# Layer 0's 64 slots written out on four engines, layer 1's left in its loop

## The chip, the core and the metric

The kernel runs on one core of a Trainium2 chip. The metric is the device time of one execution in microseconds (us). Five engines work side by side, each on its own list of instructions: TensorE (PE in the rows; PEld is its weight load), VectorE (DVE), ScalarE (ACT), GpSimd (POOL) and SyncE (SP), which issues most of the transfers. They meet only through semaphores.

## The reference, cut to what matters

Two transformer layers work on 1,024 tokens of width 256 (4 sequences of 256), all in fp32. Layer 0 is attention with 16 query heads and 8 key/value heads, an RMS norm and a rotation of queries and keys and a window of 128, and then a feed-forward part that keeps 2 of every 4 hidden values. Layer 1 is causal attention with 16 heads, and then a feed-forward part with a Walsh-Hadamard transform.

```python
x = x + _L0_attn_ref(_layernorm(x), ...)   # 16 heads in 8 pairs, 4 sequences
x = x + _L0_ffn_ref(_layernorm(x), ...)
x = x + _L1_attn_ref(_layernorm(x), ...)   # 16 heads in 8 pairs, 4 sequences
x = x + _L1_ffn_ref(_layernorm(x), ...)
```

## The kernel before

The attention of a layer is cut into 64 units: 8 pairs of heads, and in each pair 8 units (4 sequences times 2 heads). A **slot** c is one step of a software pipeline: in it every engine works on several units at once. In slot c TensorE makes the scores of unit c, projects tile c+5 of the weights (six matmuls with 512 columns, L535 in layer 0, L543 in layer 1), multiplies the probabilities of an earlier unit with the values (L465, L470, L472) and makes the output product of unit c-6 (L427). VectorE adds outputs to `x` (L734 or L743), takes the maxima of the scores (L798), splits results into a high and a low fp32r part (L754, L762, L810, L812, L859) and turns the probabilities in blocks of 32 (L774). ScalarE takes the exponentials (L713), copies results out of PSUM (L621, L635 to L639, L664, L675 to L699), and in layer 1 makes the high part of the turned probabilities (L591) and issues the transfer of the blocks (L603). GpSimd splits weights (L888, L890) and in layer 0 does a part of the rotation (L901 to L910).

Nobody schedules this at run time: each engine's list is written in the order of its slot function (`pe_slot`, `act_slot`, `dve_slot`, `pool_slot`), and waits on semaphores tie the lists together. The function `slots` (L949) writes the slots of a layer: slots -5 to 8 one after the other, then a hardware loop (`eng.Fori`, L954) with a body of 16 slots that runs 3 times (slots 9 to 56), then the rest. So each of the four engines has a loop for layer 0 and one for layer 1, with two jumps back each. In a loop the number that a wait compares with depends on the pass, so that `need` (L70 to 76) and `need_pairs` (L79 to 84) make a register operation ahead of such a wait; outside a loop it is a constant. SyncE's list has no loop in either layer.

`Fori` itself leaves rows at L954: a register set ahead of the loop (MOVE), the loop's first instruction (FUSED_REGOPS), and at its end an addition (ALU_OP) and the jump (COMPARE_BRANCH).

The sizes of the loops, counted in the built program with waits and register operations (the accumulator reads that the trace shows on ScalarE and the weight loads of TensorE included), and the place of their first and last instruction in the engine's list, counted from 0:

| engine | whole list | layer 0's loop | layer 1's loop |
|---|---|---|---|
| PE | 4,993 | 444 to 1232 (789) | 2776 to 3748 (973) |
| DVE | 1,365 | 190 to 481 (292) | 875 to 1144 (270) |
| ACT | 1,333 | 203 to 566 (364) | 871 to 1163 (293) |
| POOL | 464 | 96 to 271 (176) | 373 to 425 (53) |
| SP | 730 | none | none |

Of the kernel before, what the change touches and what calls it, by code (L numbers as in the profile page):

```python
# [36 lines left out]
UNITS = 8 * PAIRS  # L37
# [11 lines left out]
FIRST_SLOT, LOOP_FROM, LOOP_STEP, LOOPS, LAST_SLOT = -5, (9, 9), 16, 3, 70  # L49
FIRST_TAIL = UNITS - 8 + 7  # L50
# [56 lines left out]
def build(nc, x_in, wa, wax, wb, wdown0, w2t, consts, scales, shuffle, out):  # L107
    with ExitStack() as ctx:
# [839 lines left out]

        def slots(eng, L, body, head, tail):  # L949

            for c in range(FIRST_SLOT, LOOP_FROM[L]):
                body(eng, L, None, c)
                head(c)
            with eng.Fori(0, LOOPS) as it:  # L954
                for j in range(LOOP_STEP):
                    body(eng, L, it, LOOP_FROM[L] + j)
            for c in range(LOOP_FROM[L] + LOOP_STEP * LOOPS, (LAST_SLOT if L else UNITS - 1) + 1):
                body(eng, L, None, c)
                tail(c - FIRST_TAIL)

# [729 lines left out]
        @block.gpsimd  # L1690
        def _(pool):
            nc.gpsimd.memset(zero[:, :], 0.0).then_inc(s_zero, 1)
            nc.gpsimd.memset(neg_half[:, :], -0.5).then_inc(s_half, 1)
            nc.gpsimd.memset(rms_eps[:, :], RMS_EPS).then_inc(s_half, 1)
            pool.wait_ge(s_zero, 1)
            pool.wait_ge(s_half, 2)
            for t in range(2):
                ln_pool(pool, 0, t)
            pool.wait_ge(s_rope, 16)
            pool.wait_ge(s_scl, 16)  # L1700
            for a in (2, 0):
                if a == 0:
                    pool.wait_ge(s_scq, 1)
                nc.gpsimd.tensor_tensor(cos_t[:, :, a, :], cos_c, scl[:, a // 2, :].unsqueeze(1).broadcast_to([P, 2, DH]),
                                        ALU.mult).then_inc(s_cos, 1)
            ln_pool_two(pool, 0, 2)
            pool_b(pool, 0, None, 0, 0)
            slots(pool, 0, pool_slot, pool_head0, pool_tail(pool, 0))
            pool_drain0(pool)
            for t in range(4):  # L1710
                ln_pool(pool, 2, t)
            slots(pool, 1, pool_slot, pool_head, pool_tail(pool, 1))
            for n in range(2, 5):
                pool_piece_lo(pool, 1, n)
            for n in range(5, len(pieces[1])):
                if pieces[1][n][0] == "b1" and pieces[1][n - 1][0] == "b0":
                    pool.wait_ge(ff[1]["lo"], 4)
                pool_piece(pool, 1, n)
# [4 lines left out]
        def _(act):  # L1723
# [8 lines left out]
            for L in range(2):  # L1732
# [20 lines left out]
                def tail(t):  # L1753
# [10 lines left out]
                    if L == 1 and t == 7:  # L1764
                        act_function_ahead(act, ACT.Silu)

                slots(act, L, act_slot, head, tail)
                if L == 0:
                    act_drain0(act)
# [219 lines left out]
```

## Time and profile before

| what | value |
|---|---|
| time, median of 3 runs | 686.02 us (684.66 to 689.99) |
| the profiled execution | 690.5 us, its span 688.7 us |
| busy: PE, DVE, ACT, POOL | 664.8, 559.8, 445.0, 361.8 us |
| mean granted TensorE clock | 0.988 of full speed |

The profile shows one execution. A span runs from the first to the last instruction of the program. Layer 0's attention lies at about 21 to 262 us, layer 1's at about 357 to 605 us; the feed-forward parts stand behind each.

### The profile page before, as it was taken

The page shows a single profiled execution, that of the slowest core. Times are in us where ns is not written, and L with a number is a line of the kernel's source. Part 1 is how long each engine was busy: PE and PEld are TensorE (multiplying, and loading weights), DVE is VectorE, ACT ScalarE, POOL GpSimd, SP SyncE. Part 2 cuts the span into 40 slices and gives each one's busy share as a digit, 9 for nine tenths or more (in the row PEclk, how much of TensorE's full clock was granted, in tenths as well). Part 3 has the DMA queues.
Part 4 walks back from the last instruction along what each step waited for, and adds up shares of the span by engine and source line. Part 5 has one row for each costly group of instructions (what it writes and reads, how often), then busy time and mean ns, then how long its engine had stood idle before and what let it go on. Part 6 is the DMA issues. An engine that isn't in the chain of part 4 may idle for free.

```text
span 688.7 us, 16131 instructions
## 1 busy us (share of the span) xinstructions
PE 664.8 (97%) x4153; PEld 591.8 (86%) x4153; DVE 559.8 (81%) x1706; ACT 445.0 (65%) x1721; POOL 361.8 (53%) x557
## 2 busy tenths in 40 slices
PE   7999997999799998999998999999999999999998
PEld 4689996899699997888887999999999999978887
DVE  6988996899689978878866999889899988796433
ACT  4899996899689976431435676666666666764222
POOL 5999997899789973201148943425152324027000
PEclk9999999899899999999999999999999999999999
DMA  7156574666456551100024667565656655100000
GB/s 244 48 116 147 135 159 103 140 146 128 101 122 144 124 168 49 48 0 1 16 91 86 134 134 160 110 152 111 155 117 140 135 122 130 40 1 1 1 31 31
DMA packets 242574, 69.27 MB, mean 101 GB/s; under 512 B 184400, under 2 KB 238544, under 8 KB 242384
## 3 DMA queue, kind: packets, MB, share of 16 engines
q1 hardware_dynamic: 219280, 56.53, 37.2%
q10 hardware_dynamic: 23232, 12.06, 5.9%
q8 instruction: 21, 0.34, 0.2%
q14 instruction: 41, 0.34, 0.2%
HBM read 45.29 MB, written 23.27 MB: 100 GB/s over the span
## 4 chain that ended last, share of the span: by engine, by line
PE 83%; DVE 7%; issue 4%; ACT 2%; POOL 1%; DMA 1%; SPq 0%; DVEq 0%; ACTq 0%; POOLq 0%
PE bank L543 12%; PE bank L1003 12%; PE bank L427 11%; PE bank L535 11%; PE bank L564 6%; PE bank L395 5%; PE bank L470 4%; PE bank L388 4%; PE bank L472 4%; PE bank L1077 3%; PE bank L465 3%; PE bank L487 3%; PE bank L1081 3%; DVE x L743 1%; PE bank L1097 1%
## 5 line engine op out<-in xcount | busy, mean ns | idle before, releaser
L713 ACT ACTIVATE probs<-scores,negmax 128x128 f32<-128x128 f32 (+1 forms) x256 | 117.4, 473 | 16.0 <-DVE negmax L798 15.6
L621 ACT CAST enc_hi<-bank 128x256 fp32r<-128x256 f32 x128 | 48.7, 380 | 78.4 <-PE bank L472 74.7
L888 POOL TENSOR_TENSOR a_hi<-raw_a,zero 128x384 fp32r<-128x384 f32 (+1 forms) x60 | 44.9, 749 | 73.0 <-PE bank L564 73.0
L325 POOL TENSOR_TENSOR ln_r<-ln_ve,neg_half 128x1 f32<-128x1 f32 x26 | 17.0, 655 | 118.4 <-DVE ln_ve L299 118.4
L427 PE MATMUL bank<-b_hi,enc_hi 128*128 128x256 f32 x256 | 77.9, 304 | 0.5 <-DVE x L743 0.5
L774 DVE STREAM_TRANSPOSE blocks<-probs 128x384 f32<-128x384 f32 x113 | 64.8, 573 | 12.2 <-ACT probs L713 9.4
L427 PE MATMUL bank<-b_hi,enc_lo 128*128 128x256 f32 x256 | 72.1, 282 | 0.0
L427 PE MATMUL bank<-b_lo,enc_hi 128*128 128x256 f32 x256 | 71.8, 281 | 0.0
L906 POOL TENSOR_TENSOR rot_a<-rot_a,rot_b 128x384 f32<-128x384 f32 x64 | 65.2, 1019 | 8.7 <-DVE rot_b L875 8.5
L743 DVE SCALAR_TENSOR_TENSOR x<-bank,rinv,x 128x256 f32<-128x256 f32 x144 | 67.4, 468 | 2.3 <-PE bank L427 1.0
L754 DVE TENSOR_TENSOR enc_lo<-bank,enc_hi 128x256 fp32r<-128x256 f32 x128 | 53.3, 416 | 18.7 <-PE bank L395 10.1
L904 POOL TENSOR_TENSOR rms_r<-meansq,neg_half 128x3 f32<-128x3 f32 x64 | 54.8, 856 | 7.6 <-POOL meansq L901 3.8
L1160 ACT ACTIVATE gate<-bank 128x512 f32<-128x512 f32 x32 | 19.1, 598 | 58.7 <-PE bank L1003 57.9
L890 POOL TENSOR_TENSOR a_lo<-raw_a,a_hi 128x384 fp32r<-128x384 f32 (+1 forms) x60 | 53.7, 896 | 4.7
L535 PE MATMUL bank<-a_hi,xT_hi 128*128 128x512 f32 x128 | 52.3, 411 | 2.6 <-DVE rot_b L875 1.3
L713 ACT ACTIVATION_READ_ACCUMULATOR probs<-scores,negmax 128x1 f32 x256 | 54.1, 211 | 0.0
L543 PE MATMUL bank<-xT_hi,a_hi 128*128 128x512 f32 x128 | 52.3, 409 | 0.3 <-DVE xT_lo L352 0.3
L661 ACT ACTIVATE gate<-bank 128x128 f32<-128x128 f32 x192 | 50.7, 282 | 1.7 <-PE bank L535 1.7
L427 PEld LDWEIGHTS bank<-b_hi,enc_hi 128*128 128x128 f32 x256 | 48.5, 189 | 3.4 <-issue 0.9
L535 PE MATMUL bank<-a_hi,xT_lo 128*128 128x512 f32 x128 | 50.8, 399 | 0.0
L543 PE MATMUL bank<-xT_lo,a_hi 128*128 128x512 f32 x128 | 50.7, 396 | 0.0
L535 PE MATMUL bank<-a_lo,xT_hi 128*128 128x512 f32 x128 | 50.7, 399 | 0.0
(186 smaller groups left out, 2339.7 us busy)
## 6 DMA issues: line engine op xcount, KB each, us to landing
arrived<-shuffle SPq DMA_DIRECT2D x452, 48.0 KB, 2.2
shuffle<-blocks ACTq DMA_DIRECT2D x57, 192.0 KB, 2.5
shuffle<-blocks SPq DMA_DIRECT2D x56, 192.0 KB, 2.1
raw_a<-in_wa SPq DMA_DIRECT2D x40, 192.0 KB, 3.2
raw_b<-in_wb SPq DMA_DIRECT2D x16, 256.0 KB, 2.9
raw_a<-in_wa SPq DMA_DIRECT2D x32, 128.0 KB, 2.8
hid_last<-in_wax SPq DMA_DIRECT2D x2, 512.0 KB, 3.8
w_a<-in_w2t SPq DMA_DIRECT2D x1, 1024.0 KB, 4.9
```

Source lines behind the costliest of these rows:

```text
L427: mm = pe.matmul(output_bank(L, m)[:, cols], enc[l][:, h, t * P:(t + 1) * P], b_w[slot][r][:, h * D:(h + 1) * D], start=i == 0 and not (on ...
L535: mm = pe.matmul(ps[:, :], xT[l][:, g, t * P:(t + 1) * P], a_w[slot][r][:, g * 512:(g + 1) * 512], start=i == 0, stop=i == 5)
L543: mm = pe.matmul(ps[:, :], a_w[slot][l][:, g * 768 + w * P:g * 768 + (w + 1) * P], xT[r][:, g, half * 512:(half + 1) * 512], start=i == 0, ...
L661: nc.scalar.activation(gate[:, m % 2, a * DH:(a + 1) * DH], bank[PJ_BANK + m % 2][:, a * DH:(a + 1) * DH], ACT.Square, scale=float(DH) ** ...
L713: nc.scalar.activation(probs[:, c % 4, c0:c1], scores[:, c % 2, c0:c1], ACT.Exp, bias=negmax[:, c % 2, r:r + 1], scale=-1.0, accum_out=row ...
L743: nc.vector.scalar_tensor_tensor(out=x[:, m % 8, :], in0=output_bank(L, m)[:, hh * D:(hh + 1) * D], scalar=rinv[:, u, r:r + 1], in1=x[:, m ...
L754: nc.vector.tensor_tensor(enc[1][:, w % 2, dst], bank[O_BANK][:, 0:D], enc[0][:, w % 2, dst].bitcast(F32), ALU.subtract).then_inc(s["elo"], 1)
L774: nc.vector.transpose(blocks[:, c % 2, :], probs[:, c % 4, :]).then_inc(s_blocks[L], 1)
L890: nc.gpsimd.tensor_tensor(lo, src, hi.bitcast(F32), ALU.subtract).then_inc(s_lo, 1)
L904: nc.gpsimd.tensor_tensor(rms_r[:, t, :], meansq[:, m % 2, :], neg_half[:, 0:3], ALU.pow).then_inc(s["rp"], 1)
L906: nc.gpsimd.tensor_tensor(rot_a[:, m % 2, :], rot_a[:, m % 2, :], rot_b[:, m % 2, :], ALU.add).then_inc(s["radd"], 1)
L1003: mm = pe.matmul(ps[:, :], a_w[t][l][:, c0:c0 + P], xT[rr][:, g, th * 512:(th + 1) * 512], start=q == 0, stop=q == 5)
```

## The change

In layer 0, `slots` writes out slots -5 to 63 one after the other, with the same slot functions and the same head and tail functions around them; there is no loop, and each wait compares with a constant. Layer 1 goes through the code of before. The change touches the lists of TensorE, VectorE, ScalarE and GpSimd.

```diff
         def slots(eng, L, body, head, tail):
 
+            if L == 0:
+                for c in range(FIRST_SLOT, UNITS):
+                    body(eng, 0, None, c)
+                    if c < LOOP_FROM[0]:
+                        head(c)
+                    else:
+                        tail(c - FIRST_TAIL)
+                return
             for c in range(FIRST_SLOT, LOOP_FROM[L]):
                 body(eng, L, None, c)
                 head(c)
             with eng.Fori(0, LOOPS) as it:
                 for j in range(LOOP_STEP):
                     body(eng, L, it, LOOP_FROM[L] + j)
-            for c in range(LOOP_FROM[L] + LOOP_STEP * LOOPS, (LAST_SLOT if L else UNITS - 1) + 1):
+            for c in range(LOOP_FROM[L] + LOOP_STEP * LOOPS, LAST_SLOT + 1):
                 body(eng, L, None, c)
                 tail(c - FIRST_TAIL)
```

The tail functions do nothing before slot 63 but for GpSimd's, which works at slot 62 as before. The lists of the changed kernel, counted in the same way:

| engine | whole list | layer 0's loop | layer 1's loop |
|---|---|---|---|
| PE | 6,417 | none | 4200 to 5172 (973) |
| DVE | 1,815 | none | 1325 to 1594 (270) |
| ACT | 1,925 | none | 1463 to 1755 (293) |
| POOL | 683 | none | 592 to 644 (53) |
| SP | 730 | none | none |

VectorE's list where layer 0's loop begins (slot 9), before. ISA at L954 is the loop's first instruction; ISA and REGISTER_ALU at L74 are register operations of waits; waits alone are not listed.

```order
L954 UNCONDITIONAL_BRANCH
L954 ISA
L74 ISA
L74 REGISTER_ALU
L734 TENSOR_TENSOR x<-bank,x 128x256
L798 ISA scores,negmax<-bank,cst,rms_r 128x128
L798 ISA negmax 128x1
L798 ISA scores,negmax<-bank,cst,rms_r 128x256
L798 ISA negmax 128x1
```

The same list where one slot of layer 0 follows another, now.

```order
L780 RECIPROCAL rinv<-rowsum 128x2
L754 TENSOR_TENSOR enc_lo<-bank,enc_hi 128x256
L734 TENSOR_TENSOR x<-bank,x 128x256
L798 ISA scores,negmax<-bank,cst,rms_r 128x128
L798 ISA negmax 128x1
L798 ISA scores,negmax<-bank,cst,rms_r 128x256
L798 ISA negmax 128x1
```

The loop's instruction, its jump and the register operations are gone, and the operations stand in the order of before.

VectorE's list at the end of layer 0's loop, before:

```order
L774 STREAM_TRANSPOSE blocks<-probs 128x384
L74 REGISTER_ALU
L869 TENSOR_TENSOR rot_a<-bank,cos_t 128x384
L875 TENSOR_TENSOR rot_b<-bank,sin_t 128x384
L74 REGISTER_ALU
L780 RECIPROCAL rinv<-rowsum 128x2
L754 TENSOR_TENSOR enc_lo<-bank,enc_hi 128x256
L954 REGISTER_ALU
L954 COMPARE_AND_BRANCH
```

Now these operations stand as in the fence above it, with the next slot's behind them. In layer 1 nothing changes but the loop's place in the list and its line (L962 in the changed file).

## Rows read from the trace of the kernel before

**Rows 1.** The page: busy time by engine, granted clock in 40 slices, instruction queues.
```profile
PE 664.8 (97%) x4153; PEld 591.8 (86%) x4153; DVE 559.8 (81%) x1706; ACT 445.0 (65%) x1721; POOL 361.8 (53%) x557
...
PEclk9999999899899999999999999999999999999999
...
q14 instruction: 41, 0.34, 0.2%
```
**Rows 2.** Windows of time: length, busy us (instructions) by engine, clock, DMA share, GB/s.
```profile
52.20:107.20 55.00, 55.00 (x362) 50.23 (x362) 49.46 (x172) 50.42 (x240) 51.02 (x88) 1.00 0.66 145
107.20:125.30 18.10, 13.96 (x74) 12.06 (x73) 10.34 (x37) 10.38 (x48) 13.34 (x24) 0.81 0.47 103
176.40:190.30 13.90, 9.95 (x51) 8.71 (x50) 7.00 (x24) 6.96 (x32) 9.41 (x17) 0.75 0.41 90
390.30:584.90 194.60, 194.60 (x1375) 181.69 (x1374) 176.47 (x544) 128.11 (x455) 75.87 (x108) 1.00 0.60 133
```
**Rows 3.** Timeline, TensorE in layer 0: start us, us, line, operation, [idle before <- releaser].
```profile
107.14 0.39 PE L388 MATMUL bank<-qk 128*128 128x128 f32 x2
118.81 0.87 PE L487 MATMUL bank<-cst,rot_a 128*128 128x128 f32 x3 [3.99 <-DVE k_parts L812]
125.30 0.39 PE L388 MATMUL bank<-qk 128*128 128x128 f32 x2
176.38 0.44 PE L388 MATMUL bank<-qk 128*128 128x128 f32 x2
190.27 0.39 PE L388 MATMUL bank<-qk 128*128 128x128 f32 x2
```
**Rows 4.** The chain that ended last, at layer 0's first jump: start us, us, what.
```profile
110.88 0.06 DVEq L954
110.94 3.25 issue
114.19 0.06 DVEq L954
114.25 2.50 issue
```
**Rows 5.** The same chain at layer 0's second jump.
```profile
176.54 2.85 issue
179.45 2.40 issue
```
**Rows 6.** Line L954 in layer 1, 455 to 458 us: count, durations, first start.
```profile
L954 ACTq COMPARE_BRANCH  x1: 50/50/50, 455.7 to 455.7; - x1
L954 ACTq FUSED_REGOPS  x1: 50/50/50, 455.9 to 455.9; - x1
L954 DVEq COMPARE_BRANCH  x1: 63/63/63, 456.6 to 456.6; - x1
L954 DVEq FUSED_REGOPS  x1: 63/63/63, 456.9 to 456.9; - x1
```
**Rows 7.** Line L954 in layer 0, 110 to 118 us, ScalarE.
```profile
L954 ACTq COMPARE_BRANCH  x1: 54/54/54, 110.0 to 110.0; - x1
L954 ACTq FUSED_REGOPS  x1: 50/50/50, 110.3 to 110.3; - x1
```
**Rows 8.** Instruction packets (number, MB, share), 110 to 118.5 us.
```profile
q14 instruction: 3, 0.02, 1.1%
```
**Rows 9.** The same, 458 to 584 us.
```profile
q14 instruction: 1, 0.01, 0.0%
```
**Rows 10.** Timeline of a slot in layer 1 behind its first jump.
```profile
458.32 0.38 ACT L675 COPY qk<-bank 128x256 f32<-128x256 f32 x1
458.59 0.60 ACT L680 CAST k_gate<-bank 128x512 fp32r<-128x512 f32 x1
459.64 0.69 DVE L859 TENSOR_TENSOR k_last<-bank,k_gate 128x512 fp32r<-128x512 f32 x1
462.34 0.40 PE L543 MATMUL bank<-xT_hi,a_hi 128*128 128x512 f32 x1
```

## The prediction
> **What bounds the kernel now.** I read the page first. TensorE is busy 97% of the span and VectorE 81% [rows 1], so a gain has to come out of TensorE's idle time or its clock. The strip of the granted clock dips in a few slices only, two of them in layer 0's attention. Windows of time show why these two matter [rows 2]. From 52.2 to 107.2 us TensorE is busy 55.00 of 55.00 us at full clock. From 107.2 to 125.3 us it is busy 13.96 of 18.10 at a mean clock of 0.81, and from 176.4 to 190.3 us 9.95 of 13.90 at 0.75. In layer 1's slots, 390.3 to 584.9 us, it is busy all the time at full clock. So layer 0 has two holes and layer 1 has none.
>
> The timeline sizes the holes [rows 3]. A slot begins with the matmul at L388. From 125.30 to 176.38 us there are 14 slots, 3.65 us each. From 107.14 to 125.30 there are three in 18.16 us, which is 7.2 us more than 10.95. From 176.38 to 190.27 there are two in 13.89 us, 6.6 more than 7.30. In the first hole TensorE sat idle for 3.99 us waiting for VectorE (L812); what is left of the 7.2 is mostly its lower clock after that wait, the 1.2 GHz level for a part of the window.
>
> The chain of waits names the cause [rows 4, 5]. At 110.88 us stands VectorE's jump back (L954), then 3.25 us in which it waited for nothing that the profile shows, then the loop's first instruction, then 2.50 us more of the same, and only then its second. At the second jump the two gaps are 2.85 and 2.40 us. At these moments instruction packets arrive: three between 110 and 118.5 us [rows 8]. So VectorE waits for its own code.
>
> **Why there and not elsewhere.** Length alone does not decide. ScalarE's loop in layer 0 has 364 instructions and takes 0.3 us from jump to first instruction [rows 7]; VectorE's has 292 and pays 5.9. In layer 1 VectorE (270) and ScalarE (293) take 0.2 to 0.3 us [rows 6], and over the next two passes one packet arrives [rows 9]. Place does decide, by this working. The 41 packets of queue 14 have 8 KB each [rows 1]. The four lists other than TensorE's hold 3,892 instructions (the table of lists), and some are fetched again in the loop, about ten packets; 3,892 by 31 is 126, so I take 128 to a packet, an estimate. VectorE's first instruction after the jump (190) ran alone and the second waited for another packet, so a block edge lies between 190 and 191, and then at every 128th: 319, 447, 575 and so on. Layer 0's loop (190 to 481) touches four blocks, with 1, 128, 128 and 35 instructions; layer 1's (875 to 1144) three. With the same edges ScalarE's loops (203 to 566, 871 to 1163) touch three each. The one with four stalls, and those with three don't: as if four blocks stay, one of them the block ahead.
>
> **The change part by part.**
>
> 1. Layer 0's jumps go, on all four engines. Worth 7.2 + 6.6 = **13.8 us**, idle time and clock together. The slot pace of 3.65 us stays: TensorE is busy throughout [rows 2] and its matmuls don't change. The register operations of the waits go too; I cost them at nothing, since TensorE's work hides them.
>
> 2. Code that is written out has to be fetched as well. VectorE's 48 slots become about 740 instructions, six blocks in 175 us. Before, between 52.2 and 107.2 us, the lists also crossed block edges with TensorE busy throughout [rows 2]; a block is asked for while the one before it runs. I take 0; the bound above is the second gap of a jump, 2.50 us at each edge [rows 4].
>
> 3. Layer 1's loops keep their length and move in their lists, which the diff does not show. VectorE's goes to 1325 to 1594; the edges are 1343, 1471 and 1599, so three blocks, with 4 instructions to spare. I take 0. ScalarE's goes to 1463 to 1755; the edges are 1471, 1599 and 1727, so **four blocks**, with 8, 128, 128 and 29 instructions. That is the shape that stalls. So ScalarE should now stall at layer 1's two jumps.
>
> What does that cost? It resumes 3.31 us after the jump and reaches its ninth instruction 2.57 later (the gaps of [rows 4] with the instructions between). The jump is at 455.7 [rows 6], so that is 461.5 instead of about 458.3. The copies that free the projection's bank, L675 and L680, come 3.2 us late, ending at 462.4. VectorE's L859 (0.69) behind them ends at 463.1 instead of 460.3, and the next projection on TensorE, due at 462.34 [rows 10], waits 0.8. With the shorter gaps of [rows 5] it is 0.3. If ScalarE's edge lies an instruction earlier, its copy at L621 is late too and each grows by about 0.8. What is late next is the sent blocks, by about 3 us with three slots of 4 us to go. I take **1 us a jump, 2 in all**. The bounds: 0, since nothing in layer 1 is removed that could give a gain, and 6.9 a jump, which is what a stall with no slack cost in layer 0.
>
> Sum against the profiled execution: 690.5 - 13.8 + 2 = 678.7 us. That execution lies 4.5 us above the median of the runs, 686.02, so the forecast for the median is 686.0 - 11.8 = **674.2 us**.
>
> **Rivals.**
>
> A. Layer 1 stays free, because ScalarE's edges lie elsewhere: 686.0 - 13.8 = 672.2 us. Against it: ScalarE's 364 instructions fit three blocks only if an edge lies at most 20 before instruction 203, and from nearly all such places layer 1's loop now touches four. The Trainium skill speaks for this rival ("Runtime: NRT & Kernel Launch", section "Instruction fetch mechanics"): code is fetched straight ahead, mostly hidden, and only a taken branch to a place no longer held stalls, so writing loops out is preferred. By it alone the sum ends at 672.2. It counts blocks of 256 instructions, of which two are held; by that VectorE's 270 of layer 1 could not stay, but they take 0.3 us here [rows 6], so its sizes don't fit this trace. Chance 15%.
>
> B. ScalarE's stall falls on TensorE with a larger part, up to 6.9 a jump: 674 to 686, with 680 as its middle. For it: in the first hole a wait of 3.99 us brought the lower clock with it. Against: between L859's end and L543 there are 2.0 us of slack [rows 10], and in layer 1 ScalarE is busy only 128 of 195 us [rows 2]. Chance 12%.
>
> C. Slower than before: VectorE's loop of layer 1 touches a fourth block too. Four instructions to spare decide it: if the engine reads five ahead at the jump, the block behind is asked for and the first is lost. Then both engines fetch twice at each jump, on one queue; one behind the other that is up to 11 us, less 2.0 of slack, plus the 2.9 (6.9 less 4.0) that the clock and the restart took in layer 0, so 12 a jump: 686.0 - 13.8 + 24 = 696 us. Side by side it is 6.9 a jump and 686. Against: the gap behind layer 0's jump shows an instruction at a block's end running before the next block is there [rows 4]. Chance 7%, half on each side.
>
> D. The written-out code waits at its block edges: six on VectorE at 2.5 us is 15, so 686.0 - 13.8 + 2 + 15 = 689 us. Against: the crossings of before show nothing [rows 2]. Chance 4%.
>
> The forecast keeps 62%.
>
> **How the numbers follow.** The predicted time is the forecast's, 674.2. The forecast's own range is 671 to 678: ScalarE's price from 0.3 to about 3 a jump, and the spread of the runs. Rival A lies within it; B reaches to 686. A range of 670 to 681 holds the forecast, A, and the lower half of B, some 80% once the misses at its ends are taken off. 1% is 6.9 us, about what a measurement here can tell from no change: faster means below 679.2, slower above 692.9. The forecast, A and half of B, less a little for what I have not seen, give 0.80 faster; the rest of B, half of C and D give 0.15 within 1%; the rest of C and the unseen give 0.05 slower.
>
> **What would show it.** Step 1: between layer 0's head and its last slots, TensorE is busy throughout at full clock, slots stand 3.65 us apart, and the chain has no gap at a jump. Step 2: no idle time of VectorE or ScalarE that nothing explains, though packets arrive all along. Step 3: at layer 1's jumps ScalarE's first instruction comes about 3 us after its jump, with another gap within the next ten instructions; VectorE's comes within 0.3 us; TensorE loses about a microsecond in the slot after. ScalarE free at layer 1's jumps proves my edges wrong (A); gaps on VectorE there mean C; TensorE's clock falling there means B. The prediction as a whole is wrong if layer 0's pace gets longer than 3.65 us without the loop, which no row here leads me to expect.

## The result, and the profile after

The changed kernel takes 677.1 us (median of 4 runs, 676.3 to 679.2) where the kernel before, run beside it, takes 686.6 (684.7 to 690.0): a ratio of 0.986 with a 95% interval of 0.982 to 0.991. A later set of six runs gave 0.986 [0.983, 0.989], 676.5 against 686.2 us. The forecast was 674.2 with a range of 670 to 681. The profiled execution of the changed kernel took 676.3 us.

The page of the changed kernel, against [rows 1]: busy time by engine, granted clock in 40 slices, instruction queues.

```profile
span 674.5 us, 15574 instructions
...
PE 659.0 (98%) x4153; PEld 586.6 (87%) x4153; DVE 554.6 (82%) x1705; ACT 446.2 (66%) x1721; POOL 360.0 (53%) x557
...
PEclk9999999999999999999999999999999999999999
...
q14 instruction: 50, 0.41, 0.2%
```

No slice dips any more. Queue 14 brought 50 packets where it brought 41. The four lists other than TensorE's are 1,261 instructions longer, about ten packets of code; the ten or so that were fetched again in layer 0 are gone, and about as many are fetched again in layer 1 (experiments 1 and 2 show both).

Windows of time, as in [rows 2]: layer 0's slots first, then layer 1's.

```profile
52.20:228.00 175.80, 175.80 (x1153) 160.63 (x1151) 159.59 (x551) 161.35 (x769) 164.59 (x287) 1.00 0.65 142
376.00:566.00 190.00, 188.04 (x1323) 174.68 (x1322) 168.55 (x521) 124.86 (x439) 76.64 (x109) 1.00 0.60 132
```

Layer 0's two holes are gone: TensorE is busy 175.80 of 175.80 us at full clock. Its pace is not quite the 3.65 us of before, though: from about 136 us on, every second slot takes some 3.71, 0.9 us in all. There GpSimd waits for nothing, and its operations of two slots take 7.36 us, where two of TensorE's slots at 3.65 take 7.30:

```profile
194.62 0.39 PE L388 MATMUL bank<-qk 128*128 128x128 f32 x2
...
198.33 0.39 PE L388 MATMUL bank<-qk 128*128 128x128 f32 x2
...
193.93 0.61 POOL L888 TENSOR_TENSOR a_hi<-raw_a,zero 128x256 fp32r<-128x256 f32 x1
...
201.29 0.62 POOL L888 TENSOR_TENSOR a_hi<-raw_a,zero 128x256 fp32r<-128x256 f32 x1
```

In the slot between the two matmuls GpSimd's L910 ends at 197.89 us, and the weight load of L487, which reads its result, starts at 197.94. Layer 1, which had none in [rows 2], now leaves TensorE idle for 1.96 us. Where that lies, the records of the loop's own line around layer 1's first jump tell (count, durations in ns, first and last start in us; [rows 6] has the same of before):

```profile
L962 ACTq COMPARE_BRANCH  x1: 54/54/54, 438.9 to 438.9; - x1
...
L962 DVEq COMPARE_BRANCH  x1: 68/68/68, 439.8 to 439.8; - x1
...
L962 DVEq FUSED_REGOPS  x1: 63/63/63, 440.2 to 440.2; - x1
L962 ACTq FUSED_REGOPS  x1: 56/56/56, 441.9 to 441.9; - x1
```

VectorE resumes 0.35 us behind its jump as before, ScalarE 2.96 us behind its own, where it took 0.2. The chain of waits (start us, us, what) shows ScalarE there:

```profile
439.61 2.27 issue
441.88 0.06 ACTq L962
...
442.71 0.37 ACT enc_hi L621
443.08 1.72 issue
...
444.94 0.07 ACT qk L675
...
445.23 0.11 ACT k_gate L680
...
446.08 0.89 ACT probs L713 x4
...
447.20 0.07 DVE blocks L774
...
447.70 0.44 DVE x L743
...
448.81 0.95 PE bank L427 x6
```

Two gaps, as the forecast had them: one before the loop's first instruction and 1.72 us after its eighth. What follows is a longer train than the forecast followed: the exponentials (L713) are late, behind them VectorE's turn of the probabilities (L774), behind that the output added to `x` (L743), and TensorE's L427 needs the bank that L743 frees. TensorE's timeline has both waits (columns as in [rows 3]):

```profile
441.04 0.39 PE L388 MATMUL bank<-qk 128*128 128x128 f32 x2
...
445.02 0.39 PE L388 MATMUL bank<-qk 128*128 128x128 f32 x2
...
446.68 0.47 PE L543 MATMUL bank<-xT_hi,a_hi 128*128 128x512 f32 x1 [0.92 <-DVE k_last L859]
...
448.81 0.36 PE L427 MATMUL bank<-b_hi,enc_hi 128*128 128x256 f32 x1 [0.53 <-DVE x L743]
...
450.88 0.39 PE L388 MATMUL bank<-qk 128*128 128x128 f32 x2
...
510.42 0.39 PE L388 MATMUL bank<-qk 128*128 128x128 f32 x2
...
513.30 0.36 PE L427 MATMUL bank<-b_hi,enc_hi 128*128 128x256 f32 x1 [0.49 <-DVE x L743]
515.38 0.39 PE L388 MATMUL bank<-qk 128*128 128x128 f32 x2
```

A slot of 3.98 us becomes one of 5.86 (445.02 to 450.88): 1.9 us lost. At the second jump ScalarE's gaps are shorter, 2.51 and 1.28 us, the wait for L859 is gone and only that at L427 is left; the slot takes 4.96, 1.0 us lost.

**Where the time came from.** I measure a layer from its first to its last score matmul (L388) in the timelines. The profile of before that stands ahead of the prediction has 239.4 us in layer 0 and 245.6 in layer 1. A second profile of before, taken for this comparison (685.3 us, near the median), has 237.4 and 242.0. The changed kernel has 226.1 and 244.9. Against the second profile that is 11.3 us less in layer 0 and 2.9 more in layer 1, together 8.4; the spans differ by 9.0, and 0.6 lies elsewhere.

### The profile page after: what moved, and what is told of

Read it like the earlier page. It is cut to its first block, busy times and chain, and to the rows that moved or that the text cites. A ratio compares the mean times of both kernels' runs of the same rounds, so it can differ in the third digit from the quotient of the medians.

```text
span 674.5 us, 15574 instructions
## 1 busy us (share of the span) xinstructions
PE 659.0 (98%) x4153; PEld 586.6 (87%) x4153; DVE 554.6 (82%) x1705; ACT 446.2 (66%) x1721; POOL 360.0 (53%) x557
## 4 chain that ended last, share of the span: by engine, by line
PE 85%; DVE 6%; issue 4%; ACT 3%; POOL 1%; ACTq 0%; DVEq 0%; POOLq 0%
PE bank L543 12%; PE bank L1011 12%; PE bank L427 12%; PE bank L535 11%; PE bank L564 6%; PE bank L395 5%; PE bank L470 4%; PE bank L472 4%; PE bank L388 4%; PE bank L1085 3%; PE bank L487 3%; PE bank L465 3%; PE bank L1089 3%; DVE x L743 1%; ACT probs L713 1%
## 5 line engine op out<-in xcount | busy, mean ns | idle before, releaser
L713 ACT ACTIVATE probs<-scores,negmax 128x128 f32<-128x128 f32 (+1 forms) x256 | 117.5, 474 | 4.4 <-DVE negmax L798 3.3
L427 PE MATMUL bank<-b_hi,enc_hi 128*128 128x256 f32 x256 | 78.0, 305 | 1.5 <-DVE x L743 1.5
L774 DVE STREAM_TRANSPOSE blocks<-probs 128x384 f32<-128x384 f32 x113 | 64.8, 574 | 13.8 <-ACT probs L713 10.6
L427 PE MATMUL bank<-b_hi,enc_lo 128*128 128x256 f32 x256 | 72.1, 282 | 0.0
L427 PE MATMUL bank<-b_lo,enc_hi 128*128 128x256 f32 x256 | 71.8, 281 | 0.0
L743 DVE SCALAR_TENSOR_TENSOR x<-bank,rinv,x 128x256 f32<-128x256 f32 x144 | 67.4, 468 | 2.4 <-PE bank L427 1.0
L904 POOL TENSOR_TENSOR rms_r<-meansq,neg_half 128x3 f32<-128x3 f32 x64 | 54.8, 856 | 5.6 <-DVE meansq L873 1.4
L713 ACT ACTIVATION_READ_ACCUMULATOR probs<-scores,negmax 128x1 f32 x256 | 54.4, 213 | 0.0
L543 PE MATMUL bank<-xT_hi,a_hi 128*128 128x512 f32 x128 | 52.0, 407 | 1.2 <-DVE k_last L859 0.9
L427 PEld LDWEIGHTS bank<-b_hi,enc_hi 128*128 128x128 f32 x256 | 48.5, 189 | 5.2 <-issue 2.7
L543 PE MATMUL bank<-xT_lo,a_hi 128*128 128x512 f32 x128 | 50.5, 395 | 0.0
L427 PEld LDWEIGHTS bank<-b_lo,enc_hi 128*128 128x128 f32 x256 | 48.5, 189 | 2.2
L543 PE MATMUL bank<-xT_hi,a_lo 128*128 128x512 f32 x128 | 50.3, 393 | 0.0
```

The costliest lines, as they stand in the source:

```text
L427: mm = pe.matmul(output_bank(L, m)[:, cols], enc[l][:, h, t * P:(t + 1) * P], b_w[slot][r][:, h * D:(h + 1) * D], start=i == 0 and not (on ...
L543: mm = pe.matmul(ps[:, :], a_w[slot][l][:, g * 768 + w * P:g * 768 + (w + 1) * P], xT[r][:, g, half * 512:(half + 1) * 512], start=i == 0, ...
L713: nc.scalar.activation(probs[:, c % 4, c0:c1], scores[:, c % 2, c0:c1], ACT.Exp, bias=negmax[:, c % 2, r:r + 1], scale=-1.0, accum_out=row ...
L743: nc.vector.scalar_tensor_tensor(out=x[:, m % 8, :], in0=output_bank(L, m)[:, hh * D:(hh + 1) * D], scalar=rinv[:, u, r:r + 1], in1=x[:, m ...
L774: nc.vector.transpose(blocks[:, c % 2, :], probs[:, c % 4, :]).then_inc(s_blocks[L], 1)
L904: nc.gpsimd.tensor_tensor(rms_r[:, t, :], meansq[:, m % 2, :], neg_half[:, 0:3], ALU.pow).then_inc(s["rp"], 1)
```

## The experiments

Several kernels lengthen a list by a few instructions just ahead of a loop. The helper is the same in all; `AHEAD` says for which engine and layer and how many waits. The waits are on a value that was reached long ago, and two of them make one instruction, so 2 waits move a loop by one place in its list, 17 by eight. The added lines move `Fori` from L954 to L962 or L970.

```diff
+        AHEAD = {(mybir.EngineType.DVE, 0): 2}
+
+        def pad_ahead(eng, L):
+            for _ in range(AHEAD.get((eng.engine, L), 0)):
+                eng.wait_ge(s_zero, 1)
+
         def slots(eng, L, body, head, tail):
...
                 head(c)
+            pad_ahead(eng, L)
             with eng.Fori(0, LOOPS) as it:
```

### 1. Before, with one instruction ahead of VectorE's loop in layer 0

The diff above, on the kernel before. VectorE's loop now stands at 191 to 482.

> The kernel before, both loops kept, with one more instruction on VectorE ahead of layer 0's loop (a wait that is long satisfied). Theory of place (blocks of 128 instructions, a loop that touches four stalls twice at each jump): layer 0's loop now stands at 191 to 482 and touches three blocks, 128, 128 and 36, so both of its gaps vanish, layer 1 stays as it was, and the time is 686.6 - 13.3 = 673 us, without anything written out. Rival theory, that the jump and the register operations of a loop are the cost: nothing changes, 686 to 687 us.

679.7 us (median of 6, 675.8 to 682.1), 0.991 [0.987, 0.994] of before. VectorE's records at layer 0's first jump:

```profile
L962 DVEq COMPARE_BRANCH  x1: 63/63/63, 110.7 to 110.7; - x1
L962 DVEq FUSED_REGOPS  x1: 62/62/62, 111.0 to 111.0; - x1
```

The 3.3 us of [rows 4] are 0.35, and there is no second gap; the second jump reads the same. Queue 14 brought 31 packets where before had 41. One instruction that does nothing takes both holes away, so the cause is the place of the loop and not its being a loop. Not all of the expected gain is there, though: 673 us were expected. The profiled execution is the fastest of the six, 675.8 us; what made others up to 6 us longer, no profile shows. In this one layer 0 takes 228.4 us, 2.3 more than in the changed kernel. TensorE's timeline in the later slots:

```profile
192.84 0.39 PE L388 MATMUL bank<-qk 128*128 128x128 f32 x2
...
196.49 0.39 PE L388 MATMUL bank<-qk 128*128 128x128 f32 x2
...
200.29 0.39 PE L388 MATMUL bank<-qk 128*128 128x128 f32 x2
```

But for the first slots behind each jump, every second slot from 92 us on takes 3.8 us instead of 3.65. In it the weight load of L487 waits for GpSimd's rotation:

```profile
199.91 0.31 PEld L487 LDWEIGHTS bank<-cst,rot_a 128*128 128x128 f32 x3 [0.15 <-POOL rot_a L910]
```

### 2 and 3. After, with ScalarE's loop of layer 1 moved onto a block edge; and after again

The same helper on the changed kernel, which moves ScalarE's loop from 1463 to 1471, the edge:

```diff
+        AHEAD = {(mybir.EngineType.Activation, 1): 17}
```

> The changed kernel with eight more instructions on ScalarE ahead of layer 1's loop. Theory of place: its loop moves from 1463 to 1471, the edge, touches three blocks, and ScalarE's first instruction comes 0.1 to 0.3 us after each jump instead of 2.5 to 3.0; TensorE no longer loses 1.9 and 1.0 us, so the time is 677.1 - 2.9 = 674.2 us. Rival, that ScalarE's gaps come from the list having grown longer than what stays near the engine: the gaps stay, 677 us.

The changed kernel itself, on the same chip:

> The changed kernel as it is, on the same chip as the others, so that differences of 1 to 3 us can be read. Both theories: 676 to 679 us, ScalarE's two gaps at layer 1's jumps again at about 3 and 1.5 us.

With the eight instructions 674.4 us (673.0 to 674.8, 6 runs), 0.982 [0.979, 0.985]; without them 676.5 (675.9 to 677.3, 6 runs), 0.986 [0.983, 0.989]. ScalarE's records at layer 1's first jump, with them:

```profile
L970 ACTq COMPARE_BRANCH  x1: 54/54/54, 440.3 to 440.3; - x1
L970 ACTq FUSED_REGOPS  x1: 50/50/50, 440.5 to 440.5; - x1
```

0.26 us instead of 2.96, layer 1 takes 242.2 us instead of 244.9, and queue 14 brings 41 packets instead of 50. So term 3 is real and its cause is the edge. This version is the fastest of all that ran: 2.2 us faster than the change and 11.8 faster than before.

### 4. Before, with VectorE alone written out in layer 0

```diff
+            if L == 0 and eng.engine == mybir.EngineType.DVE:
+                for c in range(FIRST_SLOT, UNITS):
+                    body(eng, 0, None, c)
+                    if c < LOOP_FROM[0]:
+                        head(c)
+                    else:
+                        tail(c - FIRST_TAIL)
+                return
```

> Only VectorE's slots of layer 0 are written out; TensorE, ScalarE and GpSimd keep layer 0's loop. Theory of place: VectorE's two stalls are the whole gain, 13.3 us, and ScalarE's list is that of before, so that its loop of layer 1 touches three blocks and has no gap: 686.6 - 13.3 = 673 us, faster than the whole change. Rival, that each engine's jumps and register operations cost a part: well under 13 us of gain, 676 to 684 us.

677.5 us (675.7 to 680.0, 6 runs), 0.987 [0.984, 0.991]. Layer 0 takes 228.2 us with the same alternate slots of 3.8 as in experiment 1, layer 1 243.6. ScalarE resumes 0.25 us after layer 1's jump, as it must, its list being that of before. So VectorE's part of the change brings nearly all of it; what is missing to my expectation is the 2.3 us of GpSimd's pace, and about 1.5 us in layer 1's first slots, whose cause these runs don't show.

### 5. Experiment 1, with GpSimd written out too

The pad of experiment 1, and the branch of experiment 4 with `Pool` for `DVE`.

> The kernel before with one more instruction on VectorE ahead of layer 0's loop, and GpSimd's slots of layer 0 written out; TensorE, VectorE and ScalarE keep both loops. With the one instruction alone every second slot of layer 0 takes 3.8 us instead of 3.65, 2.3 us in all, and TensorE waits there for GpSimd (L910). If GpSimd's register operations, about five in two slots, set that pace, layer 0 takes 226.1 us from first to last score as in the whole change, instead of 228.4, and the time is about 2.3 us below that of the one instruction alone; ScalarE's list is the old one, so layer 1 has no gap: 673 to 677 us. Rival, that the register operations of the other three engines set it: layer 0 stays at 228.4 us.

675.1 us (673.6 to 678.6, 6 runs), 0.985 [0.982, 0.988]. TensorE's timeline at the place shown in experiment 1:

```profile
192.54 0.39 PE L388 MATMUL bank<-qk 128*128 128x128 f32 x2
...
196.19 0.39 PE L388 MATMUL bank<-qk 128*128 128x128 f32 x2
...
199.83 0.39 PE L388 MATMUL bank<-qk 128*128 128x128 f32 x2
```

3.65 us each again, and layer 0 takes 226.1 us as in the changed kernel. The slots of 3.8 came from GpSimd's loop: in it GpSimd makes a register operation ahead of most waits, and written out it makes none. Its rows show the place. In experiment 1 a register operation (L74) stands at 193.5 us between L901 and L904, and L904 starts 0.36 us behind L901; here it starts 0.27 behind it. GpSimd's two slots take 7.45 us there and 7.36 here. This comes back every second slot, far from any jump, so it is not the jump. TensorE, VectorE and ScalarE still loop here, which costs a few tenths of a us at each jump (slots of 3.79 and 3.76 us at the first, 3.97 and 3.75 at the second); the changed kernel loses about as much to GpSimd's pace, so that both have 226.1.

### 6. Before, with all engines but VectorE written out in layer 0

The branch of experiment 4 with `not ... == mybir.EngineType.DVE`.

> TensorE, ScalarE and GpSimd have layer 0 written out, VectorE keeps its loop (190 to 481, four blocks). Theory of place: VectorE's two stalls of 5.3 to 5.9 us stay, layer 0 takes 238 to 239 us, and ScalarE's longer list brings its stalls into layer 1, 2.9 us: 686.2 + 2.9 less a little = 687 to 689 us, slower than before. Rival, that the loops of the other engines cost a part of the 13 us: 676 to 684 us.

688.2 us (687.4 to 690.3, 10 runs), 1.002 [1.000, 1.004]. The chain at layer 0's first jump:

```profile
111.97 0.06 DVEq L962
112.04 2.85 issue
114.89 0.06 DVEq L962
114.95 2.71 issue
```

Both gaps of [rows 4] stand, layer 0 takes 237.3 us, and ScalarE's gaps in layer 1 (2.67 and 2.91 us) come on top: layer 1 takes 245.5. The change on three of the four engines, without VectorE, is worth a little less than nothing.

### 7 and 8. After, with VectorE's loop of layer 1 moved by five, and by four

The forecast gave that loop four instructions to spare. With 10 waits it stands at 1330 to 1599, one instruction in the fourth block; with 9 waits at 1329 to 1598, up to the last place of the third.

```diff
+        AHEAD = {(mybir.EngineType.DVE, 1): 10}
```

> The changed kernel with five more instructions on VectorE ahead of layer 1's loop, which then ends at 1599, one instruction past the edge between 1598 and 1599: four blocks. Theory of place: VectorE stalls at layer 1's two jumps as well, about 3 us, then 13 instructions, then another 1 to 2 us, beside ScalarE's gaps; TensorE has 2 us of slack and its clock may fall, so 3 to 7 us a jump instead of 1.5: 676.8 + 3 to 11 = 680 to 688 us. Rival, that 270 instructions stay near the engine wherever they stand: 677 us.

> The same with four more instructions: the loop ends at 1598, the last instruction of the third block. Theory of place with the edge exactly there and no reading ahead: VectorE's first instruction comes 0.3 us after each jump of layer 1, 676 to 678 us. If the engine asks for the next block a few instructions before the edge: VectorE stalls as with five more.

By five: 682.0 us (681.4 to 682.8, 6 runs), 0.994 [0.991, 0.996]. By four: 678.9 in one run. VectorE's records at layer 1's first jump, by five:

```profile
L970 DVEq COMPARE_BRANCH  x1: 68/68/68, 442.8 to 442.8; - x1
L970 DVEq FUSED_REGOPS  x1: 63/63/63, 447.0 to 447.0; - x1
```

and by four:

```profile
L970 DVEq COMPARE_BRANCH  x1: 68/68/68, 443.0 to 443.0; - x1
L970 DVEq FUSED_REGOPS  x1: 63/63/63, 443.4 to 443.4; - x1
```

4.25 us against 0.32 (3.85 against 0.30 at the second jump), and 60 packets against 50. With the five, TensorE waits longer at the same matmul as above:

```profile
448.28 0.39 PE L427 MATMUL bank<-b_hi,enc_hi 128*128 128x256 f32 x1 [2.53 <-DVE x L743]
```

The edge is exact: with the loop's last instruction at 1598 VectorE resumes at once, with it at 1599 it stalls. That costs 4.6 us by layer 1 of the two profiles (249.9 against 245.4 us; both have some 1.7 us of waits in layer 1's first slots) and 5.4 us by the medians, which come from two sets of runs (0.994 less 0.986 of 686). The second gap that was expected is hardly there: VectorE's longest unexplained pause in the 4 us behind its first instruction is 0.37 us. Running up to the last place of the third block asks for nothing that pushes the first block out; one instruction in the fourth does.

### 9 and 10. After, with ScalarE's loop moved by seven; and before again

Seven instructions leave one of ScalarE's loop in front of the edge (15 waits):

```diff
+        AHEAD = {(mybir.EngineType.Activation, 1): 15}
```

> The changed kernel with seven more instructions on ScalarE ahead of layer 1's loop, one short of the eight that took its stalls away: it stands at 1470 to 1762, with one instruction in the first of four blocks. Theory of place: two gaps as on VectorE in layer 0 before, about 2.5 to 3.3 us to the first instruction and 2.4 to 2.6 more to the second; 677 to 679 us. Rival, that the loop's start has only to come near the edge: no gap, 674 us.

677.0 us in one run. The chain at layer 1's first jump:

```profile
439.67 2.11 issue
441.77 0.06 ACTq L970
441.83 2.39 issue
444.23 0.04 ACTq L74
```

Now the first instruction, 2.8 us behind the jump, runs alone and the second waits, as VectorE's did in layer 0. With experiment 2 this puts ScalarE's edge exactly between 1470 and 1471.

The kernel before once more, for a second profile:

> The kernel before, a second profile. Theory of place: VectorE's gaps at layer 0's two jumps again, 2.9 to 3.3 and 2.4 to 2.6 us, and layer 0's scores 238 to 240 us from first to last. Open: whether the wait of 2.2 us and the lower clock in the first slots of layer 1, which cost about 3.6 us in the first profile, belong to the kernel (then they are here too, about 690 us) or come and go (then 685 to 687 us).

685.3 us. The gaps at layer 0's jumps are there, 3.03 and 2.3 us, then 2.8 and 2.9. Windows over the first hole and over layer 1's first slots:

```profile
107.50:125.00 17.50, 13.91 (x80) 12.20 (x79) 10.34 (x37) 10.96 (x51) 13.34 (x24) 0.90 0.48 107
366.00:378.00 12.00, 11.87 (x75) 10.58 (x74) 8.09 (x27) 8.60 (x31) 10.94 (x9) 1.00 0.58 117
```

The clock in the first hole is 0.90, where [rows 2] have 0.81. Counted as the prediction counts them, three slots over the first hole and two over the second, they take 16.7 and 13.5 us, 5.8 and 6.2 more than at 3.65 each: 12.0, not 13.8. In the first profile TensorE also waited 2.20 us for VectorE (L762) near 373 us, with a fall of the clock behind it (0.55 from 373 to 376 us), some 3.6 us in all, in layer 1's first slots; here it did not. Its row in the first profile:

```profile
373.25 0.96 PE L465 MATMUL bank<-turned,v_early 128*128 128x256 f32 x3 [2.20 <-DVE turned L762]
```

## Why the prediction was right, and where it was off

**The cause** was right. VectorE's two stalls at layer 0's jumps made the two holes, and they hung on the block edge: experiment 1 removes them with one instruction and leaves the loop, and layer 0 falls from 237.4 us to 228.4; experiment 6 removes everything but them, and layer 0 stays at 237.3. The last 2.3 us come only with GpSimd written out too (experiment 5).

**Term 1, 13.8 us, was too large by about 2.5.** It was read from one execution of before, of 690.5 us, and then taken off the median, 686.0. The forecast treated the 4.5 us between them as the same before and after. They were not: 1.8 lay in the holes themselves, where the clock fell further, and 3.6 in a wait of layer 1's first slots that comes and goes. The prediction's "layer 1 has none" overlooks that wait: its window for layer 1 begins at 390 us, behind it. (The strip of the clock dips in two slices, both in layer 0; the prediction's "a few" is too many.) By the second profile the term is 12.0. Layer 0 went down by 11.3, because of the next point.

**"The slot pace of 3.65 us stays", and register operations at nothing,** held nearly, and for a reason that the forecast didn't give. TensorE being busy throughout did not settle it, since GpSimd needs a little longer for two slots than TensorE: 7.45 us in its loop, 7.36 written out, against 7.30. While it has a lead nothing shows; when the lead is used up, it sets the pace. With its loop kept and the holes gone (experiments 1 and 4) that costs 2.3 us more than written out, so the register operations are at nothing only because GpSimd is written out as well. Even so every second slot from 136 us on takes 3.71 us: the prediction named a pace longer than 3.65 us as the sign that it is wrong as a whole, and this sign came, at 0.06 us a time. The cause of the holes is not touched by it; the reason given for the pace is. In before the holes let GpSimd catch up. Slots ahead of the first hole were already longer (3.77 us at 92.27, 3.79 at 99.71), and behind the second hole GpSimd had time to wait:

```profile
192.56 0.20 POOL L901 TENSOR_TENSOR meansq<-sumsq,rms_eps 128x3 f32<-128x3 f32 x1 [0.81 <-ACT gate L661]
```

**Term 2, nothing for the edges of written-out code,** was right. In the first window of the changed kernel 19 packets came in on queue 14, with TensorE busy throughout. Rival D is out.

**Term 3** was right in place and cause. ScalarE's loop touches four blocks and stalls at layer 1's two jumps, eight instructions apart as worked out; experiments 2 and 9 fix the edge to the instruction. VectorE's four spare instructions sufficed. Its size was too small: 2.9 us in the profile and 2.2 between the medians of experiments 2 and 3, where 2 was taken; the same stalls cost 2.1 to 3.6 us in the profiles of experiments 3, 6, 8 and 9. The wait at L543 came out as worked (0.92 us for a forecast of 0.8); at the second jump it was 0 instead of 0.3. The step that failed is "what is late next is the sent blocks, with slots to go": what was late next was VectorE's L743 behind the late exponentials, and TensorE's L427 waited 0.53 and 0.49 us for it. The slots grew by more than these idle times, by 0.4 and 0.5 us: matmul records overlap (those of L427 last 0.28 us and start 0.12 apart), and the idle time is counted only from the end of the last one. From one start to the next, the first matmul of L543 came 1.08 us later than in the slot before, and that of L427 0.69 later, together 1.77 of the 1.88 lost at the first jump.

**The rivals.** A (layer 1 free) is not what happened, and experiment 2 shows that its time, 672.2 us, was near what a free layer 1 gives: 674.4. The page of the Trainium skill behind it ("Runtime: NRT & Kernel Launch", section "Instruction fetch mechanics") holds in its rule, that a taken branch to a place no longer held stalls while the fetching of straight code is mostly hidden; its blocks of 256 instructions do not hold here. The trace agrees with the rule: 2.4 to 4.3 us behind such jumps, and no idle time of TensorE in 175.80 us of straight code. The prediction threw the blocks of 256 out by a wrong working: VectorE's 270 instructions can lie on two of them, and with edges at 191 and every 256th place behind it, and two blocks held, each loop of before and of the changed kernel would run free or stall just as it did. Experiment 7 decides: the edge at 1599 is the 11th of every 128 behind 191 and none of every 256, and the packets have 8 KB each. B is out: TensorE's clock stayed at full speed in layer 1 (1.00 from 376 to 566 us), and a jump cost 1.0 to 1.9 us. C did not happen, since VectorE's loop ends four places ahead of the edge, and even one that ends right at it has no stall (experiment 8); where the loop does touch a fourth block, five places further, the price is 2.3 to 2.7 us a jump (experiment 7), not 6.9 to 12.

So the miss of 2.9 us (677.1 against 674.2) is term 1's 2.5 and term 3's 0.9, less about half a us elsewhere. Still open are the waits in layer 1's first slots, up to 3.6 us, that also stand in the profiles of experiments 4, 7 and 8.

## What to carry to other kernels

A gap behind a jump that no wait explains asks for one working: the loop's place in its engine's list against the block edges, and how many blocks it touches. Moving the loop by a few instructions can bring what writing it out brings (here one instruction took 6.5 of 9.6 us), and every change of a list's length moves the loops behind it, which have to be counted again. A hole that is read from a single execution should be read from a second one before it is taken off the median. And before a pace is said to stay when a stall goes, the other engines' times for the same work should be compared with it: one that needs barely longer, like GpSimd here, may have caught up in the stall.

## What the runs showed of the hardware

- **A loop that touches four blocks of 128 instructions loses them all.** Each such loop with its two jumps adds some ten packets of 8 KB: 41 in before and 31 with VectorE's loop on three blocks; 50 after and 41 with ScalarE's on three; 60 with VectorE's on four as well. That is five a jump, which fits the loop's four blocks and one ahead. A loop on three blocks fetched nothing again: in layer 1 of experiment 2 one packet came between 443 and 568 us, in the changed kernel ten. That four blocks are held, the one ahead among them, is worked out from this and not seen directly. Four of 8 KB are 32 KB, the size that the Trainium skill gives ("Advanced Engine Details and Errata", section "ISA Cache"), with other lines than its 16 KB.
- **A jump to a block that is lost** took 2.4 to 4.3 us to the first instruction, and where one to eight instructions of it lie before an edge, 1.3 to 2.9 more at the edge; with 13 (experiment 7) no more than 0.4. A jump to a block that is held took 0.2 to 0.35 us.
- **What a stall costs depends on who is behind it.** In layer 0 a jump with stalls on VectorE cost 5 to 7 us, the fall of TensorE's clock to the 1.2 GHz level included (granted clock 0.50 from 119 to 124 us in before, behind the idle time of 3.99 us). In layer 1 ScalarE's stalls cost 0.9 to 2.1 us a jump, and VectorE's 2.3 to 2.7, although its first gap was longer there (3.85 and 4.25 us against 2.8 to 3.3 in layer 0).
- **Register operations ahead of waits are not free on GpSimd.** Its two slots of layer 0 take 7.45 us in the loop and 7.36 written out, and layer 0 takes 228.4 and 226.1 us (experiments 1 and 5).
